# Queries and keys projected at the head of PE's slot, squares ahead of the inverse norms, the mask as a PE product, feed-forward steps a slot later

## What is computed

```python
x = attn_layer(shift_tokens(x), Wqkv[i], q_scale[i], k_scale[i], Wo[i]) + x
x = ffn_layer(shift_tokens(x), ln_g[i], ln_b[i], W1[i], b1[i], W2[i], b2[i]) + x
```

## Time and profile before

| | us |
|---|---|
| three executions | 3625.44, 3625.8, 3614.98 |
| the profiled execution | 3614.92 |
| its span, first to last instruction | 3613.1 |
| busy: PE | 3220.2 |
| busy: DVE | 2776.5 |
| busy: POOL | 2595.2 |
| busy: ACT | 2372.7 |
| mean granted TensorE clock, share of full | 0.979 |

### The profile page before, as it was taken

The page is one execution under the profiler, slowest core; times in us unless marked ns, Lnnn a source line. Parts: engine busy times, 40 slices in busy tenths (PEclk is TensorE's granted clock), DMA queues, the critical chain, the costliest instruction groups (busy, mean ns, idle before and its releaser), DMA issues.

```text
span 3613.1 us, 149929 instructions
## 1 busy us (share of the span) xinstructions
PE 3220.2 (89%) x63424; PEld 2663.0 (74%) x63424; DVE 2776.5 (77%) x4403; ACT 2372.7 (66%) x4536; POOL 2595.2 (72%) x2893
## 2 busy tenths in 40 slices
PE   6889999999999999989779899999999999999997
PEld 4777777777777777777657777777777777777775
DVE  4877887788788878887458778878887888787774
ACT  4666666666676666666436666666666666666764
POOL 5877776777677777777348777767776777777773
PEclk8999999999999999999889999999999999999998
DMA  2212221221221222221102122112212212211111
GB/s 79 67 47 57 61 57 48 61 58 47 59 60 50 58 58 54 57 56 47 32 25 72 50 54 65 52 48 64 57 45 59 63 48 57 62 52 47 45 50 34
DMA packets 117857, 195.41 MB, mean 54 GB/s; under 512 B 23756, under 2 KB 36552, under 8 KB 117192
## 3 DMA queue, kind: packets, MB, share of 16 engines
q1 hardware_dynamic: 117192, 185.82, 18.8%
HBM read 33.71 MB, written 1.05 MB: 10 GB/s over the span
## 4 chain that ended last, share of the span: by engine, by line
DVE 26%; ACT 24%; PE 22%; issue 22%; POOL 3%; ACTq 0%; DVEq 0%; DMA 0%; POOLq 0%; SPq 0%
ACT sq L526 7%; DVE rotated L708 6%; DVE ss_raw L715 5%; DVE row_max L722 4%; DVE ss L718 4%; ACT qt L542 4%; PE f_ps L1009 4%; ACT s_ps L552 3%; PE s_ps L919 3%; PE o_ps L948 3%; ACT kt L547 3%; PE tr L963 3%; DVE prob L729 2%; DVE xa L748 2%; ACT ss_log L533 2%
## 5 line engine op out<-in xcount | busy, mean ns | idle before, releaser
L418 POOL TENSOR_TENSOR rotated<-rotated 128x1024 f32<-128x1024 f32 x384 | 912.6, 2376 | 48.0 <-DVE rotated L708 46.0
L424 POOL TENSOR_TENSOR prob<-prob,rden 128x512 f32<-128x512 f32 x384 | 434.1, 1131 | 710.7 <-DVE rden L740 710.7
L702 DVE TENSOR_TENSOR rotated<-qk_ps,rot 128x1024 f32<-128x1024 f32 x384 | 470.4, 1225 | 479.3 <-ACT sq L526 479.3
L447 POOL TENSOR_TENSOR rotated<-rotated,rn 128x1024 f32<-128x1024 f32 x384 | 730.5, 1902 | 30.3 <-POOL rn L439 0.2
L919 PEld LDWEIGHTS s_ps<-kt,qt 64*32 64x32 f32 x24576 | 359.5, 107 | 230.2 <-ACT s_ps L552 204.1
L708 DVE TENSOR_TENSOR rotated<-qk_ps,rot 128x512 f32<-128x512 f32 x768 | 491.1, 681 | 0.0
L919 PE MATMUL s_ps<-kt,qt 64*32 64x64 f32 x24576 | 421.5, 218 | 72.5 <-ACT s_ps L552 72.5
L715 DVE TENSOR_REDUCE ss_raw<-sq 128x16 f32<-128x1024 f32 x384 | 464.1, 1209 | 0.0
L578 ACT ACTIVATE ot<-o_ps 128x512 f32<-128x512 f32 x384 | 229.8, 598 | 325.9 <-PE o_ps L948 324.0
L963 PE MATMUL tr<-ot,wo 128*128 128x128 f32 x3072 | 419.8, 280 | 0.0
L948 PE MATMUL o_ps<-pt,vs 64*64 64x32 f32 x12288 | 392.2, 222 | 1.4 <-ACT pt L572 1.4
(11 more groups left out here) (151 smaller groups left out, 7146.9 us busy)
## 6 DMA issues: line engine op xcount, KB each, us to landing
vs<-vn SPq DMA_DIRECT2D x384, 192.0 KB
vs<-vtail SPq DMA_DIRECT2D x384, 64.0 KB, 2.3
vtail<-vn SPq DMA_DIRECT2D x384, 64.0 KB, 2.3
staging<-layer_wqkv_dram SPq DMA_DIRECT2D x72, 256.0 KB, 3.1
wo<-layer_wo_dram SPq DMA_DIRECT2D x12, 512.0 KB, 4.6
xs<-xa SPq DMA_DIRECT2D x48, 128.0 KB, 2.5
fs<-xa SPq DMA_DIRECT2D x48, 128.0 KB, 2.5
xs<-xa SPq DMA_DIRECT2D x48, 127.8 KB, 2.4
```

Source lines behind the costliest of these rows:

```text
L418: nc.gpsimd.tensor_tensor(rot_c[h], rot_c[h], rot_s[h], ALU.add).then_inc(rot_added, 1)
L424: nc.gpsimd.tensor_tensor(prob[h][:, :, :], prob[h][:, :, :], rden[h][:, :].unsqueeze(2).to_broadcast([P, 2 * PAIRS, KEYS]), ALU.mult).the ...
L447: nc.gpsimd.tensor_tensor(folded, folded, rn[:, :].unsqueeze(2).to_broadcast([P, 2 * UH, DH]), ALU.mult).then_inc(qkn_ready, 1)
L702: nc.vector.tensor_tensor(rot_c[h], src, part(0, 0, DH), ALU.mult)
```

## The change

PE does `project_qk(n + 2)` first in every slot. The mask is no longer written by ACT: PE multiplies the identity (bf16) by the mask (bf16) into s_ps ahead of the scores. ACT does `squares(n + 2)` directly behind `keys(n)`, and `first_guess(n + 1)` behind it. Spread, norm, gated, down and add come one slot later, and w2's load and w1's split two slots later. The squares are taken of 256 times the values, with the floor and the rotary tables scaled to match, and L718 gets an upper bound beside the lower one.

```diff
-SQUARE_FLOOR = 1e-24
+SQUARE_SCALE = 256.0
+SQUARE_FLOOR = 1e-24 * SQUARE_SCALE ** 2
+SQUARE_CEIL = 2.0 ** 64
-MEAN_AT, VAR_AT, SPREAD_AT, NORM_AT, GATED_AT, DOWN_AT, ADD_AT = 3, 4, 5, 6, 7, 8, 9
-TAIL = UPS + 2
+MEAN_AT, VAR_AT, SPREAD_AT, NORM_AT, GATED_AT, DOWN_AT, ADD_AT = 3, 4, 6, 7, 8, 9, 10
+TAIL = UPS + 3
...
-    return np.ascontiguousarray(0.5 * out.astype(np.float32))
+    return np.ascontiguousarray(0.5 * SQUARE_SCALE * out).astype(np.float32)
...
-                    if m == 10 and g > 0:
+                    if m == 12 and g > 0:
                         load_w2(g)
...
-                    if m == 9:
+                    if m == 11:
                         split_w1(g)
...
-                                     ACT.Square).then_inc(sq_ready, 1)
+                                     ACT.Square, scale=SQUARE_SCALE).then_inc(sq_ready, 1)
...
-            def place_mask(U):
-                act.wait_ge(dif_ready, ONE + U)
-                nc.scalar.activation(s_ps[:, :].rearrange("p (a k) -> p a k", a=PAIRS),
-                                     mask[:, min(U // 2 % TPS, 1), :].unsqueeze(1).to_broadcast([P, PAIRS, 2 * KEYS]), ACT.Copy
-                                     ).then_inc(mask_ready, 1)
...
                         queries(n)
                         keys(n)
+                    if live(p, n + 2):
+                        squares(n + 2)
                     if live(p, n + 1):
                         first_guess(n + 1)
-                    if live(p, n) and n % UPP:
-                        place_mask(n)
-                    if live(p, n + 2):
-                        squares(n + 2)
                     if live(p, n):
                         values(n)
...
-                    if m == 8:
+                    if m == 10:
                         split_w1_high(g)
...
-                nc.vector.tensor_scalar(ss[h][:, :], ss_raw[:, :], SQUARE_FLOOR, None, ALU.max).then_inc(ss_ready, 1)
+                nc.vector.tensor_scalar(ss[h][:, :], ss_raw[:, :], SQUARE_FLOOR, SQUARE_CEIL, ALU.max, ALU.min).then_inc(ss_ready, 1)
...
-                if U % UPP == 0:
-                    nc.tensor.matmul(s_ps[:, :], ident16[:, :], mask[:, 0, :].unsqueeze(1).to_broadcast([P, PAIRS, 2 * KEYS]),
-                                     start=True, stop=False, skip_group_check=True)
-                else:
-                    pe.wait_ge(mask_ready, ONE + U - U // UPP)
+                pe.wait_ge(dif_ready, ONE + U)
+                nc.tensor.matmul(s_ps[:, :], ident16[:, :], mask[:, min(t, 1), :].unsqueeze(1).to_broadcast([P, PAIRS, 2 * KEYS]),
+                                 start=True, stop=False, skip_group_check=True)
                 pe.wait_ge(kt_ready, ONE + U + 1)
...
-                    if live(p, n + 2) and after_gated:
+                    if live(p, n + 2):
                         project_qk(n + 2)
                     if live(p, n):
                         query_heads(p, n)
                         key_heads(p, n)
-                    if live(p, n + 2) and not after_gated:
-                        project_qk(n + 2)
-                    if live(p, n):
                         project_v(n)
                         scores(n)
```

More of the change, by code:

```diff
@@ L198, in build @@
         s_ready = sem("s_ready")
-        mask_ready = sem("mask_ready")
         max_ready = sem("max_ready")
@@ L487, in _ @@
             for released in (sq_ready, qt_ready, kt_ready, prob_ready, pt_ready, vn_ready, ot_ready, fd_ready, fsq_ready,
-                             fn_hi_ready, gate_ready, guess_ready, mask_ready):
+                             fn_hi_ready, gate_ready, guess_ready):
                 act.sem_inc(released, ONE)
```

## The result

The changed kernel took 3693.36 us, median of four executions (3686.49 to 3695.15), against 3625.62 us for the kernel before (3614.98 to 3632.53): a ratio of 1.0186, 95% interval 1.0158 to 1.0214, so it is slower by some 1.6 to 2.1%. Its profiled execution has a span of 3691.5 us against 3613.1.

A forecast was written before the change was run, and what follows sets the result against it. It took POOL's 7.38 us loop as the bound, with PE's slot and the late guess costing beyond it: -2.4 + 0.67 + 0.75 + 0.17 + 2.9 - 0.34 = +1.75 a round, x 48 = +84, -11: +73, 3688 us; range 3575 to 3765.

The forecast's parts named there:

- -11 us: Slots of w1's split: L718 gets in ahead of POOL's L418, saving 0.94 us 12 times, -11 us in the whole.
- POOL's loop of 7.38 us and the hold of L718: POOL's plain slot: 6.44 us of work plus 0.94 waiting, because DVE's L718 stands still while POOL's L418 runs; stays.
- PE's own slot: PE's work from start to start: sum 7.26 us, taken as 7.35, against POOL's 7.38, so no slack is left.
- The late guess: POOL's L432 waits for the guess, now behind squares on ACT, in slots 4, 6 and 9; some 200 us in all.
- +0.67, +0.75, +0.17 and +2.9: Late-guess cost in us a round: variances (slot 4) +0.67, spread (slot 6) +0.75, centre (slot 3) +0.17, down (slot 9) +2.9.
- -0.34: Slot 10: contention of POOL's L424 with DVE (1.44 instead of 1.04 us) is hidden once, -0.34 us a round.
- The whole lateness of before as gone: -2.4: Time in which DVE, ACT or PE is late for POOL, 2.4 us a round, all counted as gained by earlier squares.
- Gated a slot later ... 0: Moving gated and L397 costs nothing: POOL's 6.85 us stay, and POOL pays for L397 in either slot.
- The first (L718 comes free): Rival: L718 no longer held by L418, POOL's loop 6.44, PE alone the bound, 69.3 us a round, 3492 us; chance 0.08.
- The fourth (a larger stall at project_v): Rival: ACT still busy when query transposes end, 0.25 us in all eight slots, +96, 3784 us; chance 0.10.

The follow-up runs named there:

- after_free: Changed kernel with the bounds of the 16 sums (L711) done by a tensor_reduce with max instead of a tensor_scalar, upper bound left out: 3587.98 us, 0.9903.
- before_free: Kernel before with its lower bound of the sums (L718) done by a tensor_reduce instead of a tensor_scalar: 3514.53 us, 0.9703.
- qk_late: Changed kernel with project_qk back behind the transposes on PE, except in the slot behind gated: 3612.37 us, 0.9977.
- late_and_guess: Changed kernel with project_qk back behind the transposes and first_guess back ahead of squares; mask product and later steps stay: 3567.81 us, 0.9848.
- mask_alone: Kernel before with the mask as PE's product instead of ACT's copy, and no other part of the change: 3588.26 us, 0.9915.
- steps_alone: Kernel before with the feed-forward steps and w1's splits in their later slots, and no other part of the change: 3587.27 us, 0.9914.
- steps_early: Changed kernel with the feed-forward steps and w1's splits back in their slots of before: 3749.53 us, 1.0357.
- mask_early_act: Changed kernel with the mask written by ACT again, between exps and queries, instead of PE's product: 3712.8 us, 1.0249.

## Why the prediction was right, and where its steps were off

It said 3688 us and 3693.36 came. The mechanism is the one it named, POOL's loop with the hold in it, PE's slot at POOL's, and the guess behind the squares. That the total came within 5 us is luck in part. With -11 us spread over the rounds, a round was to grow by 1.5 us, and with the clock full it grew by 2.2 (71.44 to 73.65, the mean of the four rounds of a layer); the 17 us of clock that the changed kernel gets back, which stand nowhere in the sum, made up for about half of that. Step by step:

- **POOL's loop of 7.38 us and the hold of L718** held: 0.94 before L425 in plain slots, L711 ending with L419 and longer than before (1220 against 697 ns), as "it waits longer for the same end" says. after_free and before_free show the hold as the cause. "In every plain slot" was too wide for the kernel before: there 233 of the 384 L718 end with L418, and 117 start only when L418 is over, take 0.2 us, and L424 waits 1.0 to 1.4. In the changed kernel 371 of 384 end with L419 and 9 with L398.
- **PE's own slot** came out 7.50, not 7.35. The mask product takes 0.32 from start to start, not 0.23 (the scores behind it start later); project_qk behind weigh_values takes 1.51, not 1.40; the restart at project_v is 0.11. I had read project_qk's 1.40 in the slot behind gated, where the products before it are like it.
- **The late guess**: +0.67, +0.75, +0.17 and +2.9 were predicted, -0.34 of it hidden, 4.15 us in all. In the round shown POOL waits 0.63, 0.69, and 2.34 + 0.24; over the four rounds of a layer it is 4.1 on average, with 0.2 at L425 in the round without L398. The whole wait was to be "some 200 us" and is 178.5. The +0.75 does not follow from its own terms: 7.05 + 0.99 - 7.38 is 0.66, and 0.69 came.
- **"The whole lateness of before as gone: -2.4"** is the term that was mis-sized. The waits of L425 and L419 fell by (80.6 + 23.0) / 48 = 2.16 us, but 0.35 of that is the clock (17 / 48) and 0.2 the slots of w1's split, counted once more under the -11. Lateness proper gave about 1.6. What I ascribed it to, squares earlier by the guess and the mask, was wrong in part too: qk_late and late_and_guess show that squares first costs 45 us with everything else equal, while mask_alone gives 29 us to the mask product, which I had on the cost side, and steps_alone 30 to the later steps, which I had at nothing, 16 of them by the clock.
- **"Gated a slot later ... 0"** was the wrong step, and steps_early shows by how much: 56 us in the changed kernel, about 15 of them the clock. POOL pays for L397 in either slot, as I wrote, but in the gated one it also holds L711 and so hid, and PE stands 2.1 us instead of 0.9. In the kernel before that costs nothing as long as the clock stays full (6.85 against 6.82 behind gated); it costs where the clock falls behind it, 17 us. In the changed kernel, where PE has no room, it costs more. Of TensorE's clock the prediction says nothing, though 0.979 of full stands in the table of before.
- **-11 us in the slots of w1's split** is borne out by the trace (1035.89, no idle time before L425).
- **The rivals.** The first (L718 comes free) did not happen, but its price can be checked now: after_free has 3588, not 3492: a round of 71.2 us, not 69.3. Eight slots of 7.50 instead of 7.35 are 1.2 of these 1.9 us; the rest is not traced. The fourth (a larger stall at project_v) did not happen: 0.25 us by the row shown in a plain slot, as the sum has it.

The rule of the Trainium skill (SBUF — State Buffer, section "Who interferes with whom"), that a tensor_scalar can hold or wait for the pair of ports shared with GpSimd while a tensor_reduce does not on this chip, agrees with the runs: 1220 ns on average as the one, 187 as the other.

What stays open: how much the two orders cost only together (7 to 16 us) and by what, what made the rest of the 30 us of the later steps on the kernel before, and why the clock fell behind 14 of the 31 long waits for hid and not behind the other 17.

## What to carry to other kernels

When an instruction's duration changes from one slot to the next with the same shape, look at which other engine's instruction ends with it: here 16 numbers waited up to 2.4 us, and changing the operation was worth more than any reordering. Before moving work to the head of an in-order queue, add up the slot from start to start and ask what the moved work was covering; the 1.4 us of project_qk had covered ACT's copy of the queries. An idle total of an engine (ACT's 441 us) says nothing of the slots in which it has none, and a step that is free while an engine has room is not free in a kernel where it has none. Before two kernels are compared by their waits, look at the granted clock of both, round by round: a mean of 0.979 against 0.986 was 17 us, and the 20 us that mask_early_act lost came by way of the clock.

## What the runs showed of the hardware that I had not expected

The clock of TensorE can fall in the middle of a kernel that keeps PE busy 89% of the time: behind a wait of 2.1 us for hid in 14 of 31 cases, and behind two waits of 0.88 and 1.73 us close together in mask_early_act, each time for 3.4 us, at 0.6 to 1.8 us a time.

L711 can be passed over once more at the moment at which it becomes ready. Timelines of DVE and POOL in the changed kernel:

```profile
1049.74 2.42 DVE L711 TENSOR_SCALAR ss<-ss_raw 128x16 f32<-128x16 f32 x1
```

```profile
1049.06 0.74 POOL L410 TENSOR_TENSOR rot<-rot_base,scales 128x256 f32<-128x256 f32 x1
1049.75 2.38 POOL L419 TENSOR_TENSOR rotated<-rotated 128x1024 f32<-128x1024 f32 x1
```

It started 0.01 us ahead of L419, while L410 still ran to 1049.80, and ended at 1052.16, 0.03 behind L419. So it went in 20 of the 22 slots in which it started 0.01 or 0.02 us ahead of L419 behind an L410; in the other two it took 0.17 us. Where it came 1.2 us before the end of L398, it ended 0.03 behind L398 and did not wait for L419 (9 times, in the slots of w1's split: at 1032.40, with L398 ending at 1033.61 and L711 at 1033.64), and L425 then follows L419 without the 0.94. So an earlier start in DVE's queue is not enough, if it is earlier by 0.01 us alone.
